# Issuing the zero fills and expert weights of a two-layer attention and expert kernel from ScalarE's DMA queue

## What is computed

```python
x = L0_attn_x
xn = _layernorm(x, axis=-1)
s = _L0_attn_ref(xn, ...)          # differential attention: two softmax maps per head, out = (a1 - lam*a2) v, group norm, Wo
g = _silu(_L0_ffn_ref(xn, ...))    # 16 experts, top 2 by softmax, swiglu, and 2 shared experts
x = x + s * g
xn = _layernorm(x, axis=-1)
s = _L1_attn_ref(xn, ...)          # 16 heads of 16, rotary, causal
g = _silu(_L1_ffn_ref(xn, ...))    # 8 experts, top 1, capacity 160, gelu
x = x + s * g
```

## Time and profile before

| | before |
|---|---|
| runs | 558.34, 556.99, 555.60 us; median 556.99 |
| the profiled execution | 553.31 us, of which span 551.6 |
| PE busy | 442.6 us, 80% of the span |
| DVE, ACT, POOL busy | 59%, 34%, 33% |
| granted PE clock, mean of the span | 0.896 of 2.4 GHz |
| SP's hardware queue (q1) | 58.92 MB, packets busy 41.5% of 16 engines |

### The profile page before, as it was taken

The page is one execution under the profiler, slowest core; times in us unless marked ns, Lnnn a source line. Parts: engine busy times, 40 slices in busy tenths (PEclk is TensorE's granted clock), DMA queues, the critical chain, the costliest instruction groups (busy, mean ns, idle before and its releaser), DMA issues.

```text
span 551.6 us, 10251 instructions
## 1 busy us (share of the span) xinstructions
PE 442.6 (80%) x3600; PEld 306.0 (55%) x3600; DVE 324.5 (59%) x831; ACT 188.6 (34%) x407; POOL 184.4 (33%) x224
## 2 busy tenths in 40 slices
PE   3436897987988898899999999777495879989960
PEld 2324664653665465467777777455374556667540
DVE  2676654898888476135432336877748585732335
ACT  1100332343453364643353323221203342554212
POOL 2332300344586305004000027442705377410324
PEclk9757898998999799999999999888558797999995
DMA  7370796397588630142332344125654867200214
GB/s 227 76 138 1 180 229 203 86 220 177 157 242 202 178 82 4 41 128 91 106 106 67 97 143 134 29 65 108 144 108 103 194 172 193 89 2 6 69 33 144
DMA packets 50108, 65.87 MB, mean 119 GB/s; under 512 B 7667, under 2 KB 41331, under 8 KB 48523
## 3 DMA queue, kind: packets, MB, share of 16 engines
q1 hardware_dynamic: 47755, 58.92, 41.5%
q0 software_dynamic: 2304, 6.29, 3.7%
HBM read 42.88 MB, written 22.02 MB: 118 GB/s over the span
## 4 chain that ended last, share of the span: by engine, by line
PE 53%; DVE 18%; DMA 9%; POOL 7%; issue 6%; SPq 4%; ACT 2%; POOLq 0%; DVEq 0%; ACTq 0%
PE bank L1013 9%; PE bank L1035 7%; PE bank L908 4%; PE bank L915 3%; PE bank L842 3%; DVE work L1474 3%; PE bank L811 3%; DMA work<-work 3%; PE bank L958 3%; PE bank L936 3%; PE bank L838 3%; DMA q_parts<-work 3%; POOL x_slots L1300 3%; DVE work L1438 2%; DMA k_parts<-work 2%
## 5 line engine op out<-in xcount | busy, mean ns | idle before, releaser
L1474 DVE TENSOR_REDUCE work<-bank 128x4 f32<-128x512 f32 (+1 forms) x144 | 96.3, 687 | 67.5 <-PE bank L842 65.7
L1136 ACT ACTIVATE work<-bank 128x512 f32<-128x512 f32 x144 | 84.1, 595 | 107.6 <-PE bank L866 64.7
L838 PE MATMUL bank<-neg_ts,identb 128*128 128x512 bf16 (+1 forms) x144 | 49.7, 345 | 31.3 <-DVE work L1474 20.2
L1100 ACT ACTIVATE work<-bank 128x256 f32<-128x256 f32 (+4 forms) x131 | 51.5, 401 | 60.3 <-PE bank L908 20.7
L1264 POOL TENSOR_TENSOR work<-work 128x512 f32<-128x512 f32 (+1 forms) x20 | 21.4, 1072 | 113.9 <-ACT work L1100 113.8
L915 PE MATMUL bank<-work,cst 128*32 128x256 f32 (+1 forms) x768 | 52.1, 342 | 0.0
L908 PE MATMUL bank<-work 128*32 128x128 f32 (+1 forms) x704 | 48.8, 351 | 3.9 <-POOL work L1255 2.6
L842 PE MATMUL bank<-work 96*128 96x256 bf16 (+1 forms) x320 | 51.1, 265 | 0.0
L1035 PE MATMUL bank<-moe,work 88*128 (+1 forms) x188 | 51.0, 395 | 0.0
L1777 DVE TENSOR_TENSOR work<-work,bank 128x176 f32<-128x176 f32 x47 | 15.8, 337 | 59.4 <-ACT work L1189 59.2
L811 PE MATMUL bank<-xnT,wqkv 128*128 128x256 f32 x160 | 41.5, 411 | 2.2 <-ACT xnT L1100 2.2
(11 more groups left out here) (196 smaller groups left out, 770.3 us busy)
## 6 DMA issues: line engine op xcount, KB each, us to landing
moe<-w_in SPq DMA_DIRECT2D x27, 352.0 KB, 4.5
work<-q_parts SPq DMA_DIRECT2D x48, 128.0 KB, 4.3
x_slots<-wo SPq DMA_DIRECT2D x9, 512.0 KB, 5.3
work<-x_slots SPq DMA_DIRECT2D x31, 128.0 KB, 2.2
y_slots<-work SPq DMA_DIRECT2D x31, 128.0 KB, 1.7
q_parts<-work SPq DMA_DIRECT2D x8, 384.0 KB, 3.2
parts<-work SPq DMA_DIRECT2D x8, 384.0 KB, 3.2
moe<-f1a_in SPq DMA_DIRECT2D x4, 512.0 KB, 4.5
```

Of the source, the lines that this page charges most:

```text
L838: nc.tensor.matmul(view[:, :, half * P:half * P + P], identb[:, :], neg_ts[:, :].unsqueeze(1).to_broadcast([P, len(ms), P]), start=True, s ...
L1100: return nc.scalar.activation(dst, src, ACT.Copy)
L1136: nc.scalar.activation(pT[at % 6], a.st.bank(w)[:, :], ACT.Exp, scale=SCALE)\
L1474: nc.vector.tensor_reduce(here[:, first:first + len(ms), half], a.s.bank((b, q))[:, :].rearrange("p (m s) -> p m s", s=n), AX_X, ALU.max, ...
```

## The change

The function `bulk` moves from the block of SP to the block of ACT, with `act.dma_start` in place of `sp.dma_start`, and so does the branch that runs it in the walk over the steps. Each bulk step keeps its place in the list, now among ACT's steps. The two waits ahead of layer 1's main list on SP are removed; ACT makes them before the first bulk step of layer 1. Sizes, number and semaphores of the transfers stay.

```diff
@@ block.sync
-            def bulk(kind, at, n):
-                if kind in ("first", "second"):
-                    dst, src = ((f1a, f1a_d), (f1b, f1b_d))[kind == "second"]
-                    sp.dma_start(dst[:, at:at + n], src[:, at:at + n]).then_inc(ld["f1"], 16)
-                elif kind == "up":
-                    sp.dma_start(w13[:, at:at + n], w13_d[:, at:at + n]).then_inc(ld["w13"], 16)
-                elif kind == "down":
-                    sp.dma_start(w2[0:FH, at:at + n], w2_d[:, at:at + n]).then_inc(ld["w2"], 16)
-                else:
-                    sp.wait_ge(zeroed, 1)
...
@@ block.sync, attention
-                    elif kind == "bulk":
-                        sp.wait_ge(a.s.full, w[1])
-                        bulk(*BULK[a.n][w[0]])
@@ block.sync, before layer 1
-            m0.dn.wait_full(sp, N0 - 1)
-            sp.wait_ge(m0.sum, TILES)
@@ block.scalar
+            def bulk(kind, at, n):
...
@@ block.scalar, attention, behind "high" and ahead of "rows"
+                    elif kind == "bulk":
+                        if a.n == 1 and w[0] == 0:
+                            m0.dn.wait_full(act, N0 - 1)
+                            act.wait_ge(m0.sum, TILES)
+                        act.wait_ge(a.s.full, w[1])
+                        bulk(*BULK[a.n][w[0]])
```

More of the change, by code:

```diff
@@ L1098, in _ @@
         def _(act):
+            def bulk(kind, at, n):
+                if kind in ("first", "second"):
+                    dst, src = ((f1a, f1a_d), (f1b, f1b_d))[kind == "second"]
+                    act.dma_start(dst[:, at:at + n], src[:, at:at + n]).then_inc(ld["f1"], 16)
+                elif kind == "up":
+                    act.dma_start(w13[:, at:at + n], w13_d[:, at:at + n]).then_inc(ld["w13"], 16)
+                elif kind == "down":
+                    act.dma_start(w2[0:FH, at:at + n], w2_d[:, at:at + n]).then_inc(ld["w2"], 16)
+                else:
+                    act.wait_ge(zeroed, 1)
+                    for slots_d, first, end in ((x0_slots_d, 0, SLOT_TILES0), (x1_slots_d, SLOT_TILES0, SLOT_TILES0 + SLOT_TILES1)):
+                        j0, j1 = max(at, first), min(at + n, end)
+                        if j0 < j1:
+                            act.dma_start(slots_d[(j0 - first) * P:(j1 - first) * P, :].rearrange("(j p) d -> p j d", p=P),
+                                         zeros.unsqueeze(1).to_broadcast([P, j1 - j0, D])).then_inc(filled, 16)
             def copy(dst, src):
```

## The result

The change made the kernel slower: 565.37 us in the median against 557.66 for the kernel before, run beside it, a ratio of 1.0189 with a 95% interval of 1.0138 to 1.024. The forecast was 551.0, with 545 to 558 as the range. The profiled execution of the kernel after took 562.09 us, with a span of 560.3 against 551.6.

A forecast was written before the change was run, and what follows sets the result against it. The prediction took TensorE to be bound by row-maximum DMAs stuck behind bulk transfers in SP's in-order queue. Its terms, 3.4 + 1.5 + 1.7 + 1.4 - 2.0 = 6.0 us, took 556.99 to 551.0 us, range 545.0 to 558.0.

The forecast's parts named there:

- What bounds the kernel: Layer 0 attention: TensorE waits 12.3 us at line 863 for row maxima queued on SP behind bulk transfers not needed yet.
- first stall: TensorE's 4.30 us wait before 85.77 us: without zero fills ahead of stage and rows, gain 3.4 us (2.1 to 4.3).
- The second: TensorE's 2.60 us wait before 134.40 us would go, but VectorE is late next: gain 1.5 us (1.0 to 2.6).
- the third: TensorE's 4.58 us wait before 181.80 us: one weight load ahead of the rows goes, gain 1.7 us (0.5 to 2.3).
- The clock: After the two long stalls TensorE's granted clock was 0.62 and 0.50 of 2.4 GHz; gain 1.4 us, at most 3.7.
- rival C: All gains at their upper bounds, with ACT's issues free: 11.8 us gained, 545.2 us; chance 0.13.
- Does a second queue slow SP's?: Layer 0: judged by GpSimd's sends beside a transfer behind six loads (5.43 against 5.28 us), it need not hold loads back.
- rival A: Rows wait for the loads, not the bulk data; only SP's issue time is saved, 3.1 less 2.0: 555.9 us; chance 0.22.
- ACT: Layer 0: 39 DMA issues on ACT, at most 9.1 us exposed beside the exponentials; taken as a cost of 2.0 us.
- rival B: ACT becomes late: no issue is hidden, 16.8 us against 8.0 gained, so +8.8, 565.8 us; chance 0.12.
- Layer 1: TensorE waits longest for VectorE, 11.4 us, none for DMAs: moving eight loads gains nothing; uncovered issues cost up to 3.4 us.

The follow-up runs named there:

- gap_act0: Kernel before with layer 0's 38 bulk steps on ACT's queue, at beats between the load bursts, right behind the rows; layer 1 as before: 552.67 us, 0.994.
- p_weights0: Kernel before with only layer 0's 27 weight loads issued by ACT; zero fills and layer 1's loads stay on SP: ratio 1.0072.
- act_dummy: Kernel before with SP unchanged, plus one 1 KB DMA on ACT at each of 46 bulk steps, to a place nobody reads: 556.80 us, ratio 1.0025.

## Why the prediction was wrong, point by point

**What bounds the kernel, and what that is worth: right.** The stalls of the earlier trace rows come from bulk data in front of stages and rows. The run with it in the gaps on SP is the change as my sum imagined it, with the data really out of the way. Of the first stall of 4.30 us it left 0.96: 3.3 gained, forecast 3.4. The second went too, while the waits for VectorE (55 to 242 us) grew from 5.7 to 7.7 us: from 126 to 141 us of the kernel before PE's lead grows from 3.6 to 5.3 us, so 1.7 was kept, forecast 1.5. I under-sized the third: 1.7 forecast, but nothing of its 4.58 was left for a DMA, and PE waited 1.53 for VectorE there, so 3.05 was gained. The clock was under-sized too. The stretches behind the stalls of that run (columns as in the earlier trace rows) show the full level, 2.4 GHz, where 0.62 and 0.50 had been:

```profile
83.60:87.90 4.30, 4.22 (x52) 2.70 (x53) 2.93 (x7) 2.39 (x4) 0.00 (x0) 1.00 1.00 313
170.00:174.50 4.50, 2.97 (x37) 1.65 (x29) 2.91 (x10) 1.07 (x2) 3.51 (x4) 1.00 0.83 231
```

The same matmuls of line 863 that took PE from 85.77 to 90.13 in the kernel before take it from 83.68 to 86.56 there, and those from 181.80 to 189.12 take it from 173.43 to 178.13. That is 1.5 and 2.6 us, 4.1 in all where I forecast 1.4 and had 3.7 as the most: behind the third stall the lower level lasted until 188 us, beyond the 186 of my row. In all PE is 11 us ahead when the fourth stall ends (207.70 in place of 218.65), of the 12.4 by which the span is shorter.

Two slips in the working decided nothing. With the burst done at 83.3 at the latest, the rest of the first stall is at most 1.8, not 2.2; and rival C, at the upper bounds, has 1.5 for the second stall in place of its 2.6.

**The step that failed: "Does a second queue slow SP's?"** I answered no, from one comparison: a stage that landed in 5.43 us with GpSimd's sends beside it, and in 5.28 without. The sum then treated data on ACT's queue as gone from SP's path. Two things were wrong with it. The sends were not like the bulk data: over that stretch, 157.8 to 163.2 us of the kernel before, they took 27.5% of the engines:

```profile
q1 hardware_dynamic: 661, 1.06, 71.7%
q0 software_dynamic: 174, 0.49, 27.5%
```

ACT's queue took 44.1% beside the third burst of the kernel after. Why the sends got along is open; no run here varied them. And that comparison has no burst of loads and no set of rows in it, the two that PE waits for. For a key stage itself the answer was wrong. From issue to landing, the three key stages behind six loads took 5.3, 4.8 and 5.4 us in the kernel before and 6.4, 6.6 and 7.4 after; the last is the one that I had compared. With only layer 0's weights on ACT they took 5.4, 6.5 and 7.2: the first, which then has only zero fills beside it, on SP's own queue, stays as it was. With layer 0's data on ACT but later, behind the rows, they took 5.4, 5.3 and 6.1.

**What stood in its place.** Sharing alone is rival A, and it gives a small gain. What made the kernel slower was that SP's waits had been pacing the bulk data. I had noted that SP blocks at a load until the stage has landed and that everything stands behind it; I read it only as a cost to the critical transfers. It also kept each bulk step that stands behind a load in the list behind the whole burst, and behind the rows where those came first. It did not keep bulk data away from the stages: a zero fill at 71.35 and a weight load at 119.56 went out behind a stage and ahead of its loads, and the order that I read left them out. ACT has no such wait, so the bulk steps go out when due, into the stage, the loads or the rows. At the first stall this shows in each step of the sum: stage to loads took 4.59 us where I had taken 4.3 from 69.2 to 73.5, the stage itself was issued 1.0 later, and the three rows, issued at 79.01, released PE at 86.72, 7.7 us later, where I had them come at 81.4. The two query stages that I wanted freed did get faster, 6.20 to 4.59 and 5.60 to 3.67, but the key stages, the loads and the rows around them got slower.

**Clock: nothing came.** With the stalls still there, the mean of the granted clock was 0.894 against 0.896.

**ACT: over-priced.** 2.0 us forecast, nothing that can be told was measured. PE's wait for the exponentials at line 841 was 1.0 us in three, as before. So rival B, slower, had the sign right with the wrong mechanism; nor did an issue on ACT double beside a burst of SP's (0.30 us at 178.08).

**Layer 1: wrong.** "Moving eight transfers gains nothing" was right, but I priced only ACT's issues as a loss. That no DMA stood among PE's waits did not mean that the transfers there had room: the move cost 0.58%. And it was one execution: in three other kernels with layer 1's loads at their old place on SP (`gap_act0`, `p_weights0`, `act_dummy`) PE waited 1.5 to 1.8 us for rows in the next burst, at 482 to 487 us.

**Rival A**, that only issue time is saved, was closer than the forecast and also too low. The rule behind it, from the Trainium skill, "DMA: Bandwidth & Descriptors", section "Issuing engines are not separate DMA queues", holds in its first half here, the queues share the engines. Its second half, that more issuers only save issue time, leaves out the order that one queue gives: the runs show that taking it away costs 1.9%, and nothing that can be told when the beats are moved.

**Rival C** fell with the forecast. No rival named the mechanism that decided.

## What to carry to other kernels

Before a transfer is moved off an in-order queue, list what that queue's waits keep it behind: a queue that blocks is also a schedule, and on another queue the same steps go out earlier, beside what they used to follow. Bulk data that is needed late should be placed by time, in the gaps between the bursts that an engine waits for and behind the small transfers that end a burst; then the queue hardly matters, and here placement was worth 2.5 to 2.9% where the queue was worth nothing that can be told. An engine that has no wait for a DMA today may still have a DMA landing just in time; the slack has to be read, not the absence of a wait, and in more than one execution: the same stall differed by up to 3 us between executions that issue the same bulk data from the same queue.

## What the hardware showed that I had not expected

Issuing DMAs from a busy ScalarE was almost free: an issue takes 0.33 us in the median (0.334 to 0.381 for the 18 upper weights), less than SP's 0.43, and runs inside the activation ahead of it. The issues on ACT, of the kernel after (ns: least/median/most):

```profile
L1083 ACTq DMA_DIRECT2D moe<-w_in x18: 334/335/381, 99.5 to 173.0; - x18
```

And three DMAs of 8 KB suffer as much as large ones: alone they land in about 1.8 us, beside two queues of bulk data in 7.9 in the median.
